# Mixture-of-experts slots that begin while the last batches are still being routed

## The reference

```
x = attention(x)                 # 8 heads of 16, softmax over 1024 keys, w_out, + tokens
t = tokens(x)
u = layernorm(t)                 # spike attention: q = u Wq' >= 0.25, k = u Wk' >= 0.25, v = u Wv' >= 0.3
t = t + sum_m [causal and q.k > 0.1] v_m
xt = layernorm(t)                # experts: 8 of them, 128 -> 512 -> 128
p = softmax(xt Wr + br); route = argmax p
t = t + (gelu(xt W1[route] + b1[route]) W2[route] + b2[route]) * pmax / pmax
out = channels first again
```

## Time and profile before

| what | us |
|---|---|
| median of three timed runs | 1170.01 |
| profiled execution, first to last instruction (its span; the profile gives no other time for it) | 1184.0 |
| PE ends batch 6's logits | 968.6 |
| first slot's transpose on PE | 1012.00 |
| first slot's result on DVE | 1019.67 |
| last tell on POOL starts | 1156.69 |
| result stage, from the last tell to the end | 27.3 |

### The profile page before, as it was taken

The page is one execution under the profiler, slowest core; times in us unless marked ns, Lnnn a source line. Parts: engine busy times, 40 slices in busy tenths (PEclk is TensorE's granted clock), DMA queues, the critical chain, the costliest instruction groups (busy, mean ns, idle before and its releaser), DMA issues. The chain is left out here.

```text
span 1184.0 us, 23775 instructions
## 1 busy us (share of the span) xinstructions
PE 1083.5 (92%) x8048; PEld 532.3 (45%) x8048; DVE 878.6 (74%) x2004; ACT 779.7 (66%) x1691; POOL 323.0 (27%) x379
## 2 busy tenths in 40 slices
PE   5999999999999999999999999999888952799995
PEld 2223333333333343333333333333666642799994
DVE  4889889888988988997888898870577753355555
ACT  2167777777877777777787787778567431355563
POOL 4131041031113104103101310035225556244450
PEclk7599999999999999999999999999999875799996
DMA  5519008305503700820650470000611111222227
GB/s 132 112 47 171 22 2 179 58 8 126 112 2 79 144 16 22 177 41 1 140 98 2 92 128 3 1 20 1 158 29 33 32 33 54 57 69 69 68 60 290
DMA packets 66204, 85.53 MB, mean 72 GB/s; under 512 B 15544, under 2 KB 48952, under 8 KB 64552
## 3 DMA queue, kind: packets, MB, share of 16 engines
q1 hardware_dynamic: 60744, 72.91, 28.2%
q0 software_dynamic: 4320, 8.89, 2.2%
q10 hardware_dynamic: 1024, 2.23, 0.6%
HBM read 57.08 MB, written 26.65 MB: 71 GB/s over the span
## 5 line engine op out<-in xcount | busy, mean ns | idle before, releaser
L733 DVE TENSOR_REDUCE neg_half<-slot 128x1 f32<-128x512 f32 x1024 | 634.4, 683 | 102.6 <-PE slot L508 85.3
L647 ACT ACTIVATE probs<-ring 128x512 f32<-128x512 f32 x1024 | 528.8, 602 | 136.9 <-PE ring L517 134.6
L517 PE MATMUL ring<-stack_q,stack_k 50*128 50x512 bf16 (+1 forms) x2048 | 420.9, 383 | 2.0
L559 PE MATMUL acc<-probs,v_sb 128*32 128x512 f32 x2048 | 273.6, 606 | 0.0
L517 PEld LDWEIGHTS ring<-stack_q,stack_k 50*128 50x128 bf16 (+1 forms) x2048 | 152.4, 93 | 257.9 <-issue 110.7
L510 PE MATMUL slot<-twin_k,twin_q 48*128 48x512 bf16 x512 | 183.5, 393 | 20.0 <-DMA twin_q<-parts_dram 12.0
L508 PE MATMUL slot<-stack_k,stack_q 48*128 48x512 bf16 x512 | 162.7, 393 | 2.8 <-DVE neg_half L733 2.8
L1581 ACT ACTIVATE zt<-bank,b_of 128x128 f32<-128x128 f32 x284 | 81.2, 369 | 86.5 <-PE bank L1549 64.8
L423 POOL CAST m_parts<-neg_max 128x16 bf16<-128x16 f32 x32 | 6.3, 198 | 380.5 <-DVE neg_max L739 380.5
L1524 POOL DMA_INDIRECT rows_tok<-zt,x_in x71 | 68.3, 962 | 88.8 <-DVE zt L1609 86.3
L510 PEld LDWEIGHTS slot<-twin_k,twin_q 48*128 48x128 bf16 x512 | 47.7, 94 | 95.0 <-DVE neg_half L733 73.0
(11 more groups left out here) (161 smaller groups left out, 1121.3 us busy)
## 6 DMA issues: line engine op xcount, KB each, us to landing
parts_dram<-parts SPq DMA_DIRECT2D x30, 384.0 KB, 5.7
stack_k<-parts_dram SPq DMA_DIRECT2D x16, 384.0 KB, 6.1
stack_q<-parts_dram SPq DMA_DIRECT2D x32, 192.0 KB, 7.3
x_in<-rows_in SPq DMA_DIRECT2D x71, 64.5 KB
xp<-in_x SPq DMA_DIRECT2D x8, 512.0 KB, 4.7
stack_k<-parts_dram SPq DMA_DIRECT2D x16, 256.0 KB, 3.8
xr<-in_x SPq DMA_DIRECT2D x8, 512.0 KB, 4.1
out<-zt SPq DMA_DIRECT2D x16, 256.0 KB, 2.1
```

Source lines behind the costliest of these rows:

```text
L517: return pe.matmul(out[:, :], stack_k[s % STACK_BUFS][rows, h, kt * P:(kt + 1) * P], stack_q[s % STACK_BUFS][rows, half, h, :], start=star ...
L559: mm = pe.matmul(acc[32 * h:32 * h + 32, :], v_sb[s // G % 2][:, kt, s % G * HG + h, :], probs[:, j % PROBS, h, :], start=(kt == 0), stop= ...
L647: act.activation(probs[:, j % PROBS, h, :], ring[n % S_BANKS][:, :], ACT.Exp).then_inc(s_empty[n % S_BANKS], 1)
L733: dve.tensor_reduce(neg_half[q % 2][:, half, k:k + 1], slot[n % M_BANKS][:, :], AX.X, ALU.max, negate=True).then_inc(m_empty[n % M_BANKS], 1)
```

## The change

The experts are taken in three phases. `PREFIX = (5, 7, 8)` batches are routed when a phase's table is made, and `BOUNDS = (33, 49, 71)` are the slots that end them. Whatever the routing, 5 batches (40 tiles of rows) hold at least 40 - 7 = 33 full tiles, and 7 batches 49. So slots 0 to 32 take full tiles of the first five batches, slots 33 to 48 full tiles of the first seven, slots 49 to 70 all that is left, with the tails.

- Round 8 is gone from `STAGE`. The engines' middle programs now call the expert stage's functions for single slots, and the rest of the routing stands between slots by number: PE does sums(6) before slot 3, turn2(7) before slot 7, logits(7) before 8, sums(7) before 12. ACT does z2 of batch 7 before Gelu 5, the transposes' copies before Gelu 8, Exp of batch 7 before Gelu 9. POOL takes the root of batch 7 before tell 1, and scatters batch 6 with tells 4 to 11 and batch 7 with tells 14 to 21.
- DVE makes `table(0)` in round 6, at turn2 of batch 5, between the two counts of batch 6. weights(0) and weights(1) stand before less_max of batch 6. Then: xt(0), xt(1), choose(6) with the second half of the statistics of batch 7 and slots 0 and 1 in it, variances(7), slot 2, positions(6), slot 3, normal2(7), table(1) with slots 4 to 7 in it, less_max(7), slot 8, choose(7) with slots 9 and 10 in it, slot 11, positions(7), slot 12, table(2) with slots 13 to 16 in it, the gain, and slots 17 to 70. DVE's slot is now weights(s+2), xt(s+2), result(s).
- PE begins the slots straight behind logits of batch 6, when the six banks that it takes have been taken. The last two transposes share the seventh bank.
- `table(n)` counts full tiles (no rounding up) in phases 0 and 1, subtracts what earlier phases have taken (`done_e`) and works on its own slots alone.
- SP loads each phase's rows when that phase's table is made and its batches' scatters have landed (`s_sent` is three semaphores). Tails are sent before the last phase, behind load 48, with one register load for all eight.
- b1 lies behind w1 in one tile of 516, so that one copy brings both. b1 is loaded by eight DMAs.
- x_in and y have rings of 16, not 8 and 4. y and the hidden tile lie in `mask[0]`, not in `zt2`.

The diff, cut to its core:

```diff
+X_RING, Y_RING = 16, 16
+PREFIX = (5, 7, B)
+BOUNDS = tuple(n * KT - (E - 1) for n in PREFIX[:-1]) + (SLOTS,)
+FIRST = (0,) + BOUNDS[:-1]
+SUM_AT, Z2_AT, TURN2_AT, LOGIT_AT, SUM2_AT = 3, 4, 7, 8, 12
+SEND_AT, SEND2_AT = 4, 14
...
-STAGE += [job for r in range(-1, B + 1) for job in round_jobs(r)]
+STAGE += [job for r in range(-1, B) for job in round_jobs(r)]
+LATE = [("turn2", B - 1, j) for j in range(2)]
...
 # gpsimd
+        for k in range(4, KT):
+            scatter(B - 3, k)
+        for m in range(SLOTS):
+            if m == 1:
+                inverse_root(B - 1)
+            if SEND_AT <= m < SEND_AT + KT:
+                scatter(B - 2, m - SEND_AT)
+            if SEND2_AT <= m < SEND2_AT + KT:
+                scatter(B - 1, m - SEND2_AT)
+            tell(pool, m)
...
 # tensor
+        begin()
+        for m in range(SLOTS):
+            if m == SUM_AT:
+                sums(B - 2)
+            if m == TURN2_AT:
+                for job in LATE:
+                    turn2(job)
+            if m == LOGIT_AT:
+                logits(B - 1)
+            if m == SUM2_AT:
+                sums(B - 1)
+            slot(m)
...
 # scalar
+        gelu(0)
+        for m in range(1, SLOTS):
+            if m == Z2_AT + 1:
+                z2_of(B - 1)
+            if m == TURN2_AT + 1:
+                for job in LATE:
+                    turned(job, zt2, lambda back: act.wait_ge(s_logit, back + 1))
+            if m == LOGIT_AT + 1:
+                exp(B - 1)
+            gelu(m)
...
 # vector
+            elif kind == "turn2" and b == PREFIX[0] and args == 0:
+                table(0)
             elif kind == "logit":
+                if b == B - 2:
+                    weights_of(0)
+                    weights_of(1)
                 less_max(b)
...
+        copy_xt(0)
+        copy_xt(1)
+        choose(B - 2, beside_choice)
+        variances(B - 1)
+        slot(SUM_AT - 1)
+        positions(B - 2)
+        slot(SUM_AT)
+        normal2(B - 1)
+        table(1, lambda k: slot(Z2_AT + k))
+        less_max(B - 1)
+        slot(LOGIT_AT)
+        choose(B - 1, lambda k: slot(LOGIT_AT + 1 + k // 4) if k in (3, 7) else None)
+        slot(SUM2_AT - 1)
+        positions(B - 1)
+        slot(SUM2_AT)
+        table(2, lambda k: slot(SUM2_AT + 1 + k))
...
 # sync of the expert stage
+            if s0 in FIRST:
+                phase = FIRST.index(s0)
+                sent = PREFIX[phase] - (PREFIX[phase - 1] if phase else 0)
+                if s0 == FIRST[-1]:
+                    send_tails(sp, regs)
+                    sp.wait_ge(s_tail, 16 * (E + 1))
+                sp.wait_ge(s_table, 2 * phase + 2)
+                sp.wait_ge(s_sent[phase], 16 * KT * sent)
...
-            dve.tensor_copy(b1_of[:, s % 2, :], tile_of(b1_sb, e))
-            dve.tensor_copy(w1_of[:, s % 2, :], tile_of(w1_sb, e)).then_inc(s_w1, 1)
+            expert[s] = expert_of(s)
+            dve.tensor_copy(w1_of[:, s % 2, :], tile_of(w1_sb, expert[s])).then_inc(s_w1, 1)
```

More of the change, by code:

```diff
@@ L887, in middle_stage @@
                   slot_start, slot_row, tail_row, s_sent, s_tail, s_table, load_weights):
+    MOST = max(last - first for first, last in zip(FIRST, BOUNDS))
     w_t = sb("w_t", [P, 3, C], F32)
@@ L971, in bank_of, with send_tails, sync @@
     def bank_of(job):
-        return bank[PLACE[job] % RING]
-    def sync(sp):
+        return bank[LATE_BANK if job in LATE else PLACE[job] % RING]
+    def send_tails(sp, regs):
+        sp.wait_ge(s_pos, B + 1)
+        sp.load(regs[0:E], tail_row[0:1, 0:E])
+        for e in range(E):
+            row = sp.snap(regs[e], min_val=0, max_val=E * REGION - P)
+            sp.dma_start(rows_in[bass.ds(row, P), :], tails[:, e, :]).then_inc(s_tail, 16)
+    def sync(sp, load_slots):
         sp.dma_start(w_r[:, :], wr).then_inc(s_w, 16)
@@ L980, in sync, with gpsimd @@
                      tails[:, E:FILLERS, :]).then_inc(s_tail, 16)
[L981 to L986, removed]
+        load_slots(sp, send_tails)
+    def gpsimd(pool, tell):
         def fill(ap, value):
@@ L1016, in scatter @@
             pool.indirect_dma_start(rows_in, bass.IndirectOffsetOnAxis(ap=pos[:, t:t + 1], axis=0),
-                                    z_all[:, t, :], None).then_inc(s_sent, 16)
+                                    z_all[:, t, :], None).then_inc(s_sent[sum(b >= n for n in PREFIX)], 16)
         def inverse_root(b):
@@ L1053, in gpsimd, with tensor @@
         wait_filled(pool, ("count", B - 1, 1))
[L1054 to L1077, removed]
+        for k in range(4, KT):
[8 more added lines that the diff above has]
+            tell(pool, m)
+    def tensor(pe, begin, slot):
         def weights():
@@ L1272, in scalar, with vector @@
                 exp(b)
-    def vector(dve):
+        for j in range(2):
+            wait_filled(act, ("count", B - 2, j))
+        gelu(0)
[8 more added lines that the diff above has]
+            gelu(m)
+    def vector(dve, weights_of, copy_xt, slot):
         steps = [0]
@@ L1459, in vector, with beside_choice @@
             elif kind == "sum":
-                if b == B - 2:
-                    choose_and_spread(B)
                 positions(b)
-        table()
+        def beside_choice(k):
+            if k < KT // 2:
+                spread(B - 1, KT // 2 + k)
+            if k == KT // 2 - 1:
+                slot(0)
+            if k == KT - 1:
+                slot(1)
+        for j in range(2):
+            wait_filled(dve, ("count", B - 2, j))
+        copy_xt(0)
+        copy_xt(1)
+        choose(B - 2, beside_choice)
@@ L1472, in middle_stage @@
[L1472 to L1477, removed]
+        for m in range(SUM2_AT + 5, SLOTS):
+            slot(m)
+    others = [bank[(LATE_BANK + 1 + n) % RING] for n in range(RING - 1)]
+    free = mask[0][:, :, :].rearrange("p k n -> p (k n)").bitcast(F32)
@@ L1518, in sync, with tell @@
                 sp.dma_start(x_in[:, s % X_RING, :], rows_in[bass.ds(row[j], P), :]).then_inc(s_x[s % X_RING], 16)
[L1520 to L1526, removed]
+    def tell(pool, s):
+        pool.wait_ge(s_y, s + 1)
+        pool.wait_ge(s_x[s % X_RING], 16 * (s // X_RING + 1))
+        pool.indirect_dma_start(rows_tok, bass.IndirectOffsetOnAxis(
+            ap=x_in[:, s % X_RING, C:C + 1].bitcast(U32), axis=0), y[:, s % Y_RING, :],
+            None).then_inc(s_told[s % Y_RING], 16)
     def tensor(pe):
@@ L1560, in down, with begin, slot @@
             mm.then_inc(s_down, 1)
[L1562 to L1568, removed]
+        def begin():
+            pe.wait_ge(s_ew, 16 * (E + 3))
+            turn(0)
+            up(0)
+            turn(1)
+        def slot(s):
             if s + 1 < SLOTS:
@@ L1573, in tensor, with gelu @@
             down(s, start_of(s))
+        return begin, slot
     def scalar(act):
-        for s in range(SLOTS):
+        def gelu(s):
             act.wait_ge(s_up, s + 1)
```

191 lines of the change are left out of this document (101 added, 90 removed).

## The result

The changed kernel takes 1151.74 us (median of four, 1150.88 to 1152.89) against 1170.51 before: a ratio of 0.9832, interval 0.9815 to 0.985. It is 18.8 us faster where 25 was forecast; that is 1.6%, well beyond the 0.2% that the prediction takes as no change. The profiled execution of after spans 1148.7, for a time of 1151.01.

What follows compares the result with a forecast made beforehand. PE was taken as full in the slots, with a 43 us hole of latencies before them. 39.6 - 12.3 - 4.8 + 2.5 = 25.0 off 1170.0 gave 1145.0 us; own range 1138 to 1152, whole range 1134 to 1160.

Steps and rivals of the forecast that it cites:

- Step (a): Hole before the slots: the first up starts at 973.3 instead of 1012.9, a gain of 39.6 us.
- Step (b): Routing work added on DVE between slots 1 to 17: a cost of 12.3 us.
- step (c): Late transposes, logits and Exp of batch 7 added on PE and ACT before slots 7 to 9: 4.8 us cost.
- The cover of 0.12: DVE's loop of 1.77 beside PE's 1.89: a slot grows by the DVE time laid before it, less 0.12 us.
- Step (e): Separate b1 copy removed from DVE's slot: period 1.89 instead of 1.925, a gain of 2.5 us over 70 slots.
- (d): POOL's 16 scatters and a root between the tells: it lags by some 5 us at most and costs nothing.
- (f): Row loads of the later phases, at slots 33 and 49: counted 0, bounds 0 and 5 us.
- 1: TensorE falls to its lower clock in the stretched slots; half of it leaves a gain of 15, 1155 us; 20%.
- 2: The lower clock lasts beyond slot 17, each further slot costing 1.8 us; to slot 33, 1194 us; 3%.
- 3: Slot 49 waits for SP's tails, up to 5 us: 1150 us; 8%.
- 4: First slots start late because rows of the first five batches arrive late; 3 us beyond the 2.7 margin gives 1148; 4%.
- 5: More gain: full clock at the start (2.9 us) and a slot period of 1.83 (4.5 more): 1137.6 us; 10%.

Runs made afterwards that it cites:

- the tails experiment: The kernel before, with the eight tail rows' registers filled by one load instead of eight: 1171.37 us, ratio 1.0006.
- v_split: The changed kernel with table(0) in two parts, the second in round 7 behind the choice for batch 5: 1149.43 us, ratio 0.981.
- a_b1_apart: The changed kernel with b1 and w1 copied by two DVE instructions again: 1154.32 us, ratio 0.9845.
- v_all: The changed kernel with the edits of v_spread, v_split and v_warm together: 1145.59 us, ratio 0.9774.
- a_reg: The changed kernel with DVE's register load of a slot's expert moved from ahead of the w1 copy to behind the last result: 1151.98 us, ratio 0.9842.
- v_all_reg: v_all with DVE's register load moved in the same way as in a_reg: 1148.16 us, ratio 0.9805.
- v_warm: The changed kernel with idle bf16 matmuls on PE, 48 in round 7 and 14 behind the first transpose: 1150.0 us, ratio 0.9812.
- v_spread: The changed kernel with the routing laid thinner, at most two DVE steps between two slots: 1149.67 us, ratio 0.9819.
- a_dummy2: The changed kernel with two idle DVE copies of 512 columns added behind each of slots 24 to 43: 1154.85 us, ratio 0.9871.

## Why the prediction came out as it did

The second profile of before (1169.8) and that of after (1148.7), each taken in an execution within 1.2 us of its median, give the terms. Their spans are 21.1 apart, the medians 18.8. The forecast's column is its own sum, laid on the same marks.

| stretch | before again | after | moved | forecast |
|---|---|---|---|---|
| start to count(6,0) | 946.4 | 946.1 | -0.3 | 0 |
| count(6,0) to last count of batch 7 | 16.4 | 18.7 | +2.3 | +1.25 |
| to the first up | 36.5 | 3.3 | -33.2 | -40.9 |
| to result 0 | 6.8 | 7.0 | +0.1 | 0 |
| result 0 to 18 | 35.2 | 46.2 | +10.9 | +17.1, and -2.5 over all slots |
| result 18 to 70 | 100.5 | 98.7 | -1.8 | |
| to the end | 27.9 | 28.8 | +0.9 | 0 |
| sum | | | -21.1 | -25.0 |

**The mechanism was right**: the slots start behind batch 6's logits, the routing stretches some of them, POOL and SP hold nothing up, and the clock stays up in the stretched slots. The forecast's own range, 1138 to 1152, holds the median at its upper end, and that is in part luck: two errors worked against each other. The shift of the first up was 30.9 us (33.2 less 2.3), not 39.6, which is 8.7 too much gain, and the DVE work in the slots was priced 5.0 too high. Had the slots cost what was forecast, a shift of 30.9 would have left a gain of 16.3 and a time of 1153.7, outside that range.

**Step (a), the hole, was too large by 7.7** (40.9 against 33.2). The prediction took 43 us from one execution whose span was 14 above the timed median, and wrote "I carry the difference over unchanged and do not explain it". Most of it stood in the very place that the change removes: 8.7 in the hole. The second profile and the tails experiment show it. Against this, DVE's start was quicker than worked out: from the end of batch 7's statistics to the first up 1.7 us (966.40 to 968.08), not 2.7 (970.62 to 973.3 by the prediction's own steps), as the two w1 copies went one behind the other (0.92 for both) with their register loads hidden.

**table(0) cost 2.3, not 1.25.** The DVE idle time of 3.54 that covered it was itself of a slow round: in the profile of before taken again the second count follows the first by 1.75, with 1.07 of idling. The chain took 4.5, as worked out (4.8). v_split took 1.0 of this away.

**Step (b), DVE work between slots, was too large by 5.0.** Eighteen slots at 1.89 are 34.0; the stretch took 46.15, so 12.1 were added, 4.8 of them in slots 7 to 9, which are step (c). DVE's share is 7.3, not 12.3. The slots that PE or ACT sets came out as worked out: slot 7 3.70 (3.69 forecast), slot 8 4.23 (4.09), slot 9 2.56 (2.69). Those that DVE sets did not: slot 4 took 3.07 (3.92), slot 5 2.47 (2.62), slot 12 2.50 (3.07), slot 13 2.47 (2.97), slot 6 1.94 (2.87). Not all were shorter: slot 1 took 3.01 (2.77), and slots 11 and 18, for which the prediction has nothing, 2.39 and 2.19. The cover of 0.12, read from a slot in which each engine followed the other closely, is too small: the dummy copies were hidden to 0.6 a slot. For dependent steps the runs show 0.1 to 0.4 paid of 0.45.

**Step (e)** was right in size (1.8 in the 52 full slots, 2.5 forecast for 70) and wrong in its reason, as a_b1_apart shows. Which of the other edits gives the steadier 1.89 (deeper rings, the order of the loads) was not tried.

**Steps (c), (d), (f)** held: PE's insertions as above (4.8 in sum, as forecast); tells start at most 4.4 us behind their results (tell 21) and catch up by tell 27; no wait on x_in at slots 33 or 49.

**Rivals.** 1 and 2 did not happen in the stretched slots (0.98); in four of the other kernels (v_split, v_all, a_reg, v_all_reg) the clock fell for one slot behind the logits, some 1.5 us each. 3 did not happen. 4 did not happen in after, but its margin was smaller than the 2.7 us of the prediction: the first load left SP at 964.28, and the transpose of its rows started at 966.82, 2.5 later and straight behind the logits; in before it followed its load by 1.9 and 2.0. 5 did not happen: the first up ran at the lower clock (2.05), and the period came to 1.90, the forecast's 1.89 and not the rival's 1.83.

## What to carry to other kernels

Where the profiled execution is longer than the timed ones by more than their spread, profile again before a gap in it is priced. Here 8.7 of the 14 us of surplus lay in the very wait that the change removes. Taking dependent routing from an idle stretch into full slots costs its steps there at something between nothing and their length; here about half (7.3 us for 13.9 of steps, by the prediction's own lengths). Three further edits paid together 6 us of 1150, clear of the noise: to lay the steps thin, to split the one long chain that stood between two counts, and to keep TensorE active while it waits for a start. Alone each gave 1 to 2.5 us in its trace, and its timed runs can't be told from those of the changed kernel. Keeping TensorE active did not hold the clock up in every execution.

## What the runs showed of the hardware

- The lower clock came inside a stretch in which PE was busy all the time: behind 16 float32 matmuls of 8 columns each (the logits), one slot ran at 0.53 in v_split, and at the lower clock too in a_reg (0.56 to 0.59), v_all (0.57) and v_all_reg (0.50), each of these slots 5.7 to 5.9 us long, but not in after, v_warm, v_spread, a_dummy2 or a_b1_apart (4.23), though the logits are the same instructions in all. Why is open.
- With the same 62 idle bf16 matmuls ahead of the first up, the clock stood at 1.00 in the first slots of v_warm and v_all and at 0.50 in those of v_all_reg.
- Exp to Gelu on ACT cost 1.28 and no more in after. The table load ahead of an Exp that waits for DVE ran before the wait (993.84 against 996.44); that ahead of the first Gelu ran only behind its wait of 2.21 for PE (970.23).
- Eight SP transfers with addresses from registers took 16.2 and about 8.1 us in two executions of the same kernel, with a register load each, and 4.0 to 4.5 with one load for all.
